# One add of 2048 columns written as eight adds of 256 columns, in a graph network kernel on one core

## The reference, cut to what matters

```python
msg = jax.nn.relu(x[src] + edge_attr)          # 106250 x 256, x is xn here
agg = jnp.zeros_like(x).at[dst].add(msg)       # 6250 x 256
h = x + agg
```

## Time and profile before

| what | value |
|---|---|
| three timed runs | 2623.16, 2623.18, 2633.58 us, median 2623.18 |
| span of the profiled execution, first to last instruction | 2627.9 us, 4.7 us above that median |
| mean granted TensorE clock | 0.815 |
| busy over the span | PE 72%, DVE 46%, POOL 48%, ACT 31% |
| the edge stage | from about 93 to about 1437 us |

### The profile page before, as it was taken

How to read it: one execution, slowest core, us unless ns; L and a number is a source line. 1 busy time by engine, 2 the same in 40 slices (tenths; PEclk the granted TensorE clock), 3 DMA queues, 4 the chain that set the end, 5 groups by cost and what they waited for, 6 DMA issues and landing times. The chain is left out here.

```text
span 2627.9 us, 43936 instructions
## 1 busy us (share of the span) xinstructions
PE 1897.2 (72%) x12178; PEld 1621.3 (62%) x12179; DVE 1206.7 (46%) x3382; ACT 818.4 (31%) x1643; POOL 1251.6 (48%) x1126
## 2 busy tenths in 40 slices
PE   3566677677665677677775889663429999999993
PEld 3455555446555666566665778552318888888883
DVE  5444444445444554454454344563315445445441
ACT  5122222222221222222222345622314444444441
POOL 1566677667666766666664000225752222222221
PEclk7677788778777887777777899556759999999997
DMA  9555555546455665565554800667932232232234
GB/s 207 181 173 170 169 183 185 166 162 205 160 168 173 197 203 178 176 201 174 185 188 138 252 0 0 179 162 195 261 91 41 44 48 45 44 48 45 44 48 114
DMA packets 234810, 368.27 MB, mean 140 GB/s; under 512 B 96291, under 2 KB 184245, under 8 KB 221332
## 3 DMA queue, kind: packets, MB, share of 16 engines
q1 hardware_dynamic: 147689, 205.63, 25.4%
q0 software_dynamic: 74288, 155.59, 22.2%
q10 hardware_dynamic: 12795, 6.60, 1.3%
HBM read 286.51 MB, written 74.69 MB: 137 GB/s over the span
## 5 line engine op out<-in xcount | busy, mean ns | idle before, releaser
L497 POOL DMA_INDIRECT gathered<-xn_rows,src_index x824 | 908.5, 1103 | 433.6 <-issue 262.7
L729 PE MATMUL bank<-dst_select,message 128*128 128x128 f32 x3328 | 530.9, 318 | 278.4 <-issue 149.2
L729 PEld LDWEIGHTS bank<-dst_select,message 128*128 128x128 f32 x3328 | 494.4, 230 | 359.8 <-issue 291.1
L1637 PE MATMUL bank<-rowsT_parts,expert_weights 128*128 128x256 f16 x3564 | 409.5, 274 | 10.1 <-issue 6.2
L1604 POOL DMA_INDIRECT output_rows<-expert_out,token_index x108 | 167.7, 1553 | 475.3 <-DVE token_index L1757 446.5
L1637 PEld LDWEIGHTS bank<-rowsT_parts,expert_weights 128*128 x3564 | 346.1, 98 | 59.8 <-issue 18.0
L620 ACT ACTIVATE message<-message 128x2048 f32<-128x2048 f32 x104 | 198.7, 1910 | 522.6 <-DVE message L576 327.8
L576 DVE TENSOR_TENSOR message<-gathered,edge_attr 128x2048 f32<-128x2048 f32 x104 | 238.4, 2292 | 201.0 <-DMA gathered<-xn_rows,src_index 171.3
L1650 PE MATMUL bank<-expert_weights,gated_parts 128*128 x1836 | 209.3, 273 | 0.6 <-DVE gated_parts L1752 0.6
L1744 DVE SCALAR_TENSOR_TENSOR gated<-bank,silu 128x512 f32<-128x512 f32 x216 | 120.7, 559 | 163.7 <-ACT silu L1682 162.7
L1650 PEld LDWEIGHTS bank<-expert_weights,gated_parts 128*128 128x128 f16 x1836 | 179.5, 98 | 21.7 <-issue 0.9
(11 more groups left out here) (254 smaller groups left out, 2225.1 us busy)
## 6 DMA issues: line engine op xcount, KB each, us to landing
edge_attr<-in_edge_attr SPq DMA_DIRECT2D x104, 1024.0 KB
dispatched_rows<-empty_row SPq DMA_DIRECT2D x2, 7410.0 KB, 35.7
rows<-dispatched_rows SPq DMA_DIRECT2D x55, 260.0 KB
gathered<-xn_rows,src_index POOLq DMA_INDIRECT x832
xnT_tile<-xnT SPq DMA_DIRECT2D x100, 125.0 KB
raw_weights<-in_L_ffn_w SPq DMA_DIRECT2D x16, 640.0 KB
out<-output_rows SPq DMA_DIRECT2D x1, 6250.0 KB, 21.8
rows_to_send<-token_rows ACTq DMA_DIRECT2D x10, 568.8 KB
```

Of the source, the lines that this page charges most:

```text
L497: pool.indirect_dma_start(out=GA[h][:, e, :], out_offset=None, in_=k.xn_d[:, :], in_offset=bass.IndirectOffsetOnAxis(ap=IDX[h][:, e:e + 1] ...
L729: last = pe.matmul(PE_[h][:, c * WIN:(c + 1) * WIN], MSG[h][:, e, c * 128:(c + 1) * 128], SEL[h][:, e, :], start=e == 0, stop=e == EK - 1)
L1637: last = pe.matmul(bank[:, jj * TT:(jj + 1) * TT], w(e, wp, at + b * step, 128), X16[h][:, xp, b, :], start=n == 0, stop=n == 3 * CB - 1)
```

## The change

The add of line 576 is made in eight instructions, one for each of the eight edges of a partition, 256 columns each. The semaphore `added` is raised by the last of them.

```diff
-                    dve.tensor_tensor(MSG[h][:, :, :], GA[h][:, :, :], EA[h][:, :, :], ALU.add).then_inc(added, 1)
+                    for e in range(EK):
+                        last = dve.tensor_tensor(MSG[h][:, e, :], GA[h][:, e, :], EA[h][:, e, :], ALU.add)
+                    last.then_inc(added, 1)
```

## The result

The changed kernel takes 2782.7 us (2773.1 to 2791.4 in four runs) beside 2628.4 us before: 1.059 times as long, 95% interval 1.054 to 1.065. The forecast was 2558 us. It is outside the range and on the other side.

The account below looks back on a forecast made before the run. POOL, gathering or waiting all through the stage, was taken as the bound. 2627.9 - 80 (holds) + 9 + 6 (late places) = 2563 us for the span, 2558 us for a timed run; range 2525 to 2590, with rival B to 2625.

Parts of the forecast that it names:

- The holds: POOL's gathers held until line 576's add ends: 123 us, of which 24 stay; 5 us more from other adds.
- the sign that I had named: Sign of being right: no gather over about 1.4 us beside line 576, where they now reach 3.06.
- rival A: Gathers stay held through all eight pieces of the add, to the end of the eighth: 2670 us, chance 0.13.
- DVE's price: Eight adds on DVE end after 2.74 us, 0.45 later than one; the successor starts after 2.64 us, against 2.21.
- What is late next: Next bound at a pitch of some 10.2 us: DVE, PE and DMAs can do 8.1; PE is nearest, costing 6 us.
- the late places: The 20 places in the edge stage where POOL waits for DVE, itself waiting for PE's window sums; kept at 20.
- the 9 + 6 us for late places: Added cost: 20 uncovered places at 0.45 us, 9 us; half of 0.95 us at 13 other PE waits, 6 us.
- Rival B: The gain is given back as PE's late places become more or longer: 2601 us, 2590 to 2625, chance 0.13.
- my own sign: Sign set for the gain being given back: gathers short and POOL's waits grown by 60 us or more.
- the 65 us that I forecast: Net gain forecast for the span: 80 us of holds that count, less 9 and 6 us for late places.

Follow-up runs that it names:

- the run with two memsets: The changed kernel with two memsets of 512 columns on POOL ahead of each batch's gathers, some 1.2 us: 2770.7 us, ratio 1.040 to the kernel before.

## Why the prediction was wrong

**The holds: right.** The mean gather fell to 971 ns (I said some 980). 800.0 - 780 leaves 20 us of holds, where I had 24 and 5. Of 824 gathers only one took over 1.4 us; that none does was the sign that I had named. POOL does get its turn between two pieces, so rival A is out.

**DVE's price: right.** Eight adds take 2.77 us to the end of the last and 2.69 to the copy behind them (1399.03 to 1401.72); I took 2.74 and 2.64.

**What is late next: this step failed.** I kept the late places at 20 and asked only whether PE, DVE and the DMAs can do a batch in 8.1 us. They can, and the run with half the gathers does it all through. What I took as given is that PE's slow stretches come with the work, as many as before. They come with the gathers, and their number hangs on how these follow each other. With a hold of 1.2 us in each batch there is a stretch every five batches, 34 us after POOL resumes; with the hold shortened, to eight pieces or only to two, there is one in nearly every two, 10 us after POOL resumes. So the holds had been a brake. That it works through the pitch alone, 11.25 us against 10.3, doesn't fit the run with two memsets; how it works is not shown. POOL's waits for DVE rose by 246 us (166.5 to 412.7) where I had some 25, and its idle time of all kinds by 243; that eats the 108 us of holds and 135 more. In the sum it is the 9 + 6 us for late places that were far too small.

**Rival B** named this place ("the 20 late places become more or longer") and three more of them as its price, and bounded it at no gain. It had no bound there: 26 more came. By my own sign, short gathers and POOL's waits up by 60 us or more, what happened is B, at a size that I had ruled out. I had seen that PE "was given its instructions slowly" and that its cause was not in the trace, and still let its number be a constant of the kernel. A cost with an unknown cause belongs in the range on both sides.

**The size of the gain without stretches.** On the chip that shows none, two pieces gave 91 us, and eight pieces with 0.66 us of pause 54 us; taking the 104 x 0.66 = 69 us of pause off gives some 2358 us for eight alone, 123 less than 2481. The two kernels of eight pieces with less loaded took 2360.0 and 2363.5 us there, which fits. That is more than the 65 us that I forecast, and more than the 108 us of holds. The figure is worked out: the changed kernel was not run on that chip, and the kernel before was not profiled on it, so whether it has stretches there is not known.

**What stays open:** what the gathers and the instructions of PE and SP have in common, why the chips differ, and why eight adds at the pitch of one have twice the stretches.

## What to carry to other kernels

When an engine starts its instructions at a fixed slow beat and waits for nothing, find out what that beat depends on before making anything around it faster; a pause ahead of the suspected source is a cheap test, and here it was also the cure (eight adds with 1.8 us of pause are 3.8% faster than the kernel before). A wait that a change removes may be the brake that keeps another limit out of reach, so price the next limit as it will be without that wait. Look also at what an engine in trouble does to the one that troubles it: here nearly each stretch ended when POOL had been made to stop, and POOL's stops are what the time shows. And a gain or a loss of a few per cent may belong to the chip: the same edit in two pieces was 3.7% faster on one chip and 4.9% slower on another.

## What the runs showed of the hardware

- A gather that meets a DVE add with two SBUF inputs gets its turn at the end of that instruction, also when the next such add follows at 0.336 us (2.69/8) and the two overlap by 0.08: the mean gather takes 971 ns beside eight pieces and 1103 beside one add.
- PE can fall to one instruction every 0.70 us, for 10 to 30 us as a rule. On four chips this began some 10 us into an unbroken run of indirect gathers of 128 rows (eight of them) in the changed kernel, and ended 2.6 us behind the run's last one (medians). A fifth chip didn't show it with the same eight gathers in 10.5 us.
- SP's register instructions take 0.7 us in place of under 0.1 in the same runs, and also at 12.6 and 13.7 us a batch, where PE is free of it.
- Left out of the stage, 0.9 MB a batch of plain loads changed nothing in PE's stretches (46 against 47); half the gathers left out ended them, and SP's slow instructions too (1 of 958).
